# Announcing a landed batch of gathers three gathers later: the layer-1 edge pass of a two-layer graph network on one Trainium2 core

## The reference, cut to what matters

```python
x = (feature @ W).reshape(n, H, C)
a_src = jnp.einsum('nhc,hc->nh', x, att_src)
a_dst = jnp.einsum('nhc,hc->nh', x, att_dst)
...
e = jax.nn.leaky_relu(a_src[src] + a_dst[dst], NEG_SLOPE)
m = jax.ops.segment_max(e, dst, num_segments=n)
ex = jnp.exp(e - m[dst])
denom = jax.ops.segment_sum(ex, dst, num_segments=n)
alpha = ex / denom[dst]
msg = x[src] * alpha[:, :, None]
out = jax.ops.segment_sum(msg, dst, num_segments=n)
```

## Time and profile before

| | |
|---|---|
| median of 3 runs | 4117.95 us (4102.49 to 4120.58) |
| profiled execution | 4114.04 us |
| its span, first to last instruction | 4112.1 us |
| POOL busy with the 784 gathers of L2275 | 750.3 us |
| first and last start of these gathers | 2855.6 and 3904.7 us |
| mean granted clock of PE over the span | 0.797 |

### The profile page before, as it was taken

The page is one execution under the profiler, slowest core; times in us unless marked ns, Lnnn a source line. Parts: engine busy times, 40 slices in busy tenths (PEclk is TensorE's granted clock), DMA queues, the critical chain, the costliest instruction groups (busy, mean ns, idle before and its releaser), DMA issues. The chain is left out here.

```text
span 4112.1 us, 52958 instructions
## 1 busy us (share of the span) xinstructions
PE 2606.6 (63%) x10366; PEld 1782.4 (43%) x10367; DVE 2899.6 (71%) x5690; ACT 1696.3 (41%) x4708; POOL 2339.4 (57%) x2265
## 2 busy tenths in 40 slices
PE   0399956666666666631688886774556667676652
PEld 0155534444434443410566664553344455454432
DVE  5544435588888888897689885664566677777767
ACT  2244423344434434423344443442444444455553
POOL 4322247777777777721344444444766777777750
PEclk9999977766777767755899998997667777788876
DMA  6366689989989889831877771113566666767642
GB/s 207 108 252 265 256 293 316 317 280 285 282 280 289 278 276 288 286 122 29 256 235 234 237 227 38 34 34 60 163 176 178 190 194 193 198 192 195 189 149 83
DMA packets 602723, 839.48 MB, mean 204 GB/s; under 512 B 157060, under 2 KB 499464, under 8 KB 595936
## 3 DMA queue, kind: packets, MB, share of 16 engines
q0 software_dynamic: 123664, 438.12, 34.2%
q1 hardware_dynamic: 466170, 386.51, 30.4%
q10 hardware_dynamic: 12686, 12.72, 1.0%
HBM read 547.47 MB, written 290.84 MB: 204 GB/s over the span
## 5 line engine op out<-in xcount | busy, mean ns | idle before, releaser
L1087 POOL DMA_INDIRECT rows<-kv,kvi x880 | 942.0, 1070 | 296.8 <-issue 237.4
L2275 POOL DMA_INDIRECT g_rows<-x1t,srci x784 | 750.3, 957 | 320.3 <-issue 224.5
L1163 PE MATMUL psD<-qs,hot 128*128 x1760 | 710.9, 546 | 324.9 <-DVE prod L1375 243.8
L1163 PEld LDWEIGHTS psD<-qs,hot 128*128 128x128 f32 x1760 | 428.6, 269 | 552.6 <-issue 493.5
L2451 PE MATMUL g_psM<-g_wv,g_hot 128*128 128x264 f32 x1760 | 579.3, 485 | 103.3 <-DVE g_wv L2577 89.5
L2451 PEld LDWEIGHTS g_psM<-g_wv,g_hot 128*128 128x128 f32 x1760 | 395.7, 236 | 198.0 <-issue 115.9
L1751 PE MATMUL psM<-wv,vhot 128*128 128x260 f32 x1760 | 429.7, 393 | 81.2 <-ACT wv L1700 57.7
L1375 DVE TENSOR_TENSOR prod<-rows,psD 128x512 f32<-128x512 f32 x440 | 300.3, 682 | 251.6 <-DMA rows<-kv,kvi 210.1
L1247 ACT ACTIVATE off<-psB,npiota 128x256 f32<-128x256 f32 x440 | 206.8, 470 | 586.3 <-PE psB L1150 585.5
L1751 PEld LDWEIGHTS psM<-wv,vhot 128*128 128x128 f32 x1760 | 322.1, 190 | 188.8 <-issue 80.4
L1670 POOL TENSOR_TENSOR wv<-vrows,wgt 128x1024 f32<-128x1024 f32 x110 | 231.7, 2106 | 284.2 <-DVE vhot L1779 198.2
(11 more groups left out here) (463 smaller groups left out, 4899.7 us busy)
## 6 DMA issues: line engine op xcount, KB each, us to landing
val_v<-rows SPq DMA_DIRECT2D x220, 512.0 KB, 4.8
vrows<-val_v SPq DMA_DIRECT2D x220, 512.0 KB
sums_v<-g_run SPq DMA_DIRECT2D x110, 528.0 KB
g_drow<-drow_v SPq DMA_DIRECT2D x55, 512.0 KB
rows<-kv,kvi POOLq DMA_INDIRECT x880, 4.9
g_rows<-x1t,srci POOLq DMA_INDIRECT x784
xs<-in_x ACTq DMA_DIRECT2D x12, 896.0 KB, 11.4
g_ndt<-nodeb SPq DMA_DIRECT2D x440, 6.0 KB
```

Of the source, the lines that this page charges most:

```text
L1087: nc.gpsimd.indirect_dma_start(out=rows[:, k], out_offset=None, in_=table, in_offset=bass.IndirectOffsetOnAxis(ap=index[:, i * SLOTS + k:i ...
L1163: nc.tensor.matmul(psD[:, 2 * (V % 2) + j, 0:D], hot[:, V % 2, j * P:(j + 1) * P], node[:, ds(blk[V % 4], 1)].rearrange("p o d -> p (o d)" ...
L2275: nc.gpsimd.indirect_dma_start(out=rows[:, K % (2 * RA)], out_offset=None, in_=dr["x1t"], in_offset=bass.IndirectOffsetOnAxis(ap=v["srci"] ...
```

## The change

The announcement of batch m-1 moves from behind the third gather of batch m to behind the sixth. Nothing is added or removed: 784 gathers, 98 announcements and 92 reuse waits stay, and the number of gathers that may be in the air is still bounded by the ring alone.

```diff
                         nc.gpsimd.indirect_dma_start(
                             out=rows[:, K % (2 * RA)], out_offset=None, in_=dr["x1t"],
                             in_offset=bass.IndirectOffsetOnAxis(ap=v["srci"][:, K:K + 1], axis=0)).then_inc(got[m % RM], 16)
-                        if k == 2 and m:
+                        if k == 5 and m:
                             landed(m - 1)
                 landed(NM - 1)
```

## The result

With the announcement behind the sixth gather the kernel takes 4055.07 us (median of 4 runs, 4051.54 to 4055.84), against 4115.58 us before (4 runs, 4102.49 to 4120.58). The ratio is 0.9856, with a 95% interval of 0.9832 to 0.988: 1.4% faster. The span of the profiled execution fell from 4112.1 to 4053.8 us, by 58.3 us.

A forecast was written before the change was run, and what follows sets the result against it. POOL's gathers and their waits for landings were taken to bound the layer-1 pass. 4114.0 - 60 (landing waits) + 5 (ring) = 4059 us, or 4063 on the median's base; forecast 4061 us, range 4042 to 4088.

The forecast's parts named there:

- The bound: Layer-1 pass, 1050.1 us: as long as POOL's 784 gathers with gaps (990 us) and their waits for landings (60 us).
- The landing waits, minus 60 us: POOL's 38 gaps that end with a landing: six gathers in front of the announcement hide them all, saving 60.0 us.
- The limit of T + 7.1 us: Latest landing that six gathers would still hide, T being the end of a batch's last gather; 7.9 less 0.76 hand-over.
- The announcement, 0: POOL's instruction stream runs ahead, so late landings are still announced at the landing: 0; other end 3.8 us later each.
- The ring, plus 5 us: Gathers waiting for weightings to free their slots: without pauses they come closer, costing 12 x 0.4 = 5 us (bounds 0 to 34).
- the twelve places: Batches with under 3 us between the weighting that frees slots and the first gather; 0.4 us charged for each.
- The consumers, 0: Engines behind POOL's announcements: none becomes the bound; DVE's wait for score copies shrinks from 255 to about 200 us.
- The sum: Whole kernel: 4114.0 - 60 + 5 = 4059 us, 4063 on the runs' median; forecast 4061 us, 1.4% faster, chance 0.81.
- the first: Rival: the reuse wait takes over and the whole 34 us comes back, about 4088 us; chance 0.10.
- The second: Rival: the pause only moves, the seventh gather waiting as the fourth did, 4114 us, no change; chance 0.06.
- The third: Rival: landings come later without pauses, 49 batches costing 2.0 us each, 4152 us, slower; chance 0.03.
- The page's rule: GpSimd-issued transfer: 2.0 us plus bytes at 436 GB/s, an estimated 2.3 us per gather, making the saving 0, not 60.

The follow-up runs named there:

- the series over the places: Announcement behind the first, third (kernel before), fourth and eighth gather of the next batch: 4256.18, 4115.58, 4061.57 and 4056.02 us.
- doubled saves: SP saves the running sums twice, the second time into an unread buffer: 4106.98 us (0.998) with the third gather, 4063.52 us (0.9877) with the sixth.
- the eighth place: Against the kernel before, announcement behind the eighth gather, directly ahead of the next batch's reuse wait: 4056.02 us, ratio 0.9846.
- the four places: Against the kernel before, announcement behind the first, fourth, fifth or eighth gather: ratios 1.034, 0.9866, 0.9854 and 0.9846.
- the swap: SP issues the row flags ahead of g_drow and its eight small loads: 4058.2 us (0.9864) with the third gather, 4047.32 us (0.9846) with the sixth.
- the dummies on DVE: Three dummy DVE instructions before each chunk's first pair of weightings: 4085.73 us (0.994) with the third gather, 4080.29 us (0.9927) with the sixth.

## Why the prediction was right, by its steps

- **The bound.** Right: 784 gathers and their gaps are the pass. After the change the pass is 991.7 us of POOL's time with next to no wait in it.
- **The landing waits, minus 60 us.** Right in size and in kind. All went, and the series over the places (a loss of 207, 60, 7 and 0 us) is what cover alone would give. The limit of T + 7.1 us was not tested from above: the latest landing of any run came at T + 6.9 us, with doubled saves and the sixth gather.
- **The announcement, 0.** Right. In the kernel after five announcements of the 98 came over 0.2 us behind the landing, at most 1.0 us, by the trace's semaphore events. At the eighth place they are eight, at most 2.6 us, and the total is no longer than at the sixth.
- **The ring, plus 5 us.** Mis-sized, by a step that did not hold: it cost under 1 us. I had let a whole pause come off the distance between weighting and gather. Of the twelve places only five closed in, to between 0.8 and 1.1 us; seven moved apart, to between 2.7 and 4.2 us. At the place of the earlier trace rows the pause of 2.6 us took 1.3 us off, from 2.19 to 0.90, and nothing waited where I had put 1.2 us. So the weightings moved too; why, is not shown. The tightest place in the kernel after, DVE's pair of weightings and the first gather of the next batch:

```profile
3257.18 1.28 DVE L2577 TENSOR_TENSOR g_wv<-g_rows,g_psW 128x512 f32<-128x512 f32 x2
```

```profile
3259.26 1.09 POOL L2275 DMA_INDIRECT g_rows<-x1t,srci  x1 [0.46 <-issue]
```

  The pair ends at 3258.46, the gather starts 0.80 us later, after an idle 0.46 us: the wait has just begun to bite, by 0.16 us. In the kernel before this batch had 2.19 us, like the one in the earlier trace rows. The hand-over of 0.76 us that I took from the earlier trace rows fits. Doubled saves show what lies behind that edge: 2.3 us in one gap.
- **The consumers, 0.** Right: DVE's wait for score copies fell from 255 to 185 us, where I had said some 200.
- **The sum.** 4061 forecast, 4055 measured: the ring's 5 us are most of the difference.
- **The rivals.** Of the first, only the edge showed. The second (the pause only moves) is out by the line of the kernel after and by the four places. The third (landings get later without pauses) did not happen: no gap that ends with a landing is longer than the ordinary one, and the latest landing is where it was, at T + 6.1 us. My reason for it, that pauses let the queue drain between SP's saves, was half right: SP's transfers do make the landings late, but by where they start.
- **The page's rule.** The 2.3 us that I estimated for such a transfer from the Trainium skill's page "DMA: Bandwidth & Descriptors", section "Anatomy of one DMA — SWDGE (gpsimd) path", spoke against the change. The trace comes near it for the 56 batches with neither transfer in front of T (a median of 1.85 us after T, so 2.8 us after the last gather's start), and not for the 40 with g_drow there (4.79 us after T); the rule has no term for other queues.

That SP's order makes the landings late is shown by the swap. How the transfers delay the gathers' last rows is not. The Trainium skill's page "DMA: Bandwidth & Descriptors", section "Queues, rings and completion order", says that each DMA engine serves the rings that have work in turn, packet by packet. That would fit that twice the bytes did not delay a landing much more; no run here shows the turns. Nor do the runs separate g_drow from the eight small loads that always follow it. That the dummies on DVE cured 25 of the 38 waits by moving g_drow is what the batches' times say (5 such batches in place of 40); no run moved it by that little alone.

## What to carry to other kernels

When an engine issues work and also waits for its landing, count how much work stands between the issue and the wait, and compare it with the latest landing, not the usual one: four gathers covered nearly everything here, three lost 60 us, one lost 207. Then ask why the late ones are late; a transfer of another queue that starts at the same moment each turn can be moved for the same gain. And check a total against the wait that was meant to explain it: one of these experiments hit its range for a reason that its own profile refutes.

## What the runs showed of the hardware that was not expected

- Twice the bytes in SP's saves (110 more transfers of 528 KB) cost the kernel before nothing (0.998), while starting g_drow 4 us behind the save, in place of 0.4, is worth 1.4% (0.9864).
- The dummies on DVE, each with two operands in on-chip memory, slow the gathers beside them: with 165 of them, 687 ns each, a gather took 985 ns in place of 960. With the sixth gather 125 gathers overlap a dummy and take 1081 ns on average, those beside neither a dummy nor g_hotT 948 ns. The Trainium skill says that POOL's memory interface is shared with VectorE instructions that have two such inputs (page "GPSIMD Engine Reference", section "1. Specifications"); the trace agrees, with 19 us over 784 gathers. Two operands are not the only case: in the kernel before, the 83 gathers beside DVE's instruction that forms g_hotT from g_drow, with one tensor operand, took 1041 ns, the others 947.
- POOL's instruction stream is far enough ahead of the engine that a wait written behind the eighth gather of a batch cost nothing that could be told from the sixth (0.9846 and 0.9856).
